# A macaron block on one core: the norms' shift moved to GpSimd, weight statistics on TensorE, and a new order of the slots

## The reference, cut to what matters

```
x: 16 x 256 x 256 f32
def layernorm(x): return (x - mean) / sqrt(var + 1e-5)              # over the last 256
def ternary(w):   scale = mean(|w|) + 1e-8; return clip(round(w/scale), -1, 1) * scale
def ffn(x):       return (silu(x @ ternary(W_up).T) * (x @ ternary(W_gate).T)) @ ternary(W_down).T   # 256 -> 1024 -> 256
def attn(x):      # 16 heads of 16, rope on q and k, causal mask, softmax
    return softmax(rope(x@wq) . rope(x@wk) / 4 + mask) @ (x@wv) @ wo
x = x + 0.5 * ffn(layernorm(x))
x = x + attn(layernorm(x))
x = x + 0.5 * ffn(layernorm(x))
```

## Time and profile before

| | |
|---|---|
| median of 3 runs | 773.08 us (772.38 to 777.07) |
| the profiled execution | 772.13 us |
| its span, first to last instruction | 770.0 us |
| busy share of the span | PE 81%, DVE 79%, ACT 78%, POOL 66% |
| mean granted TensorE clock | 0.952 |

### The profile page before, as it was taken

One profiled execution on the slowest core, in us unless ns is written; L12 is line 12 of the kernel. 1 busy time (PEld: TensorE's weight loads), 2 busy tenths in 40 slices (PEclk: granted clock), 3 DMA queues, 4 the chain that ended last, 5 costly groups with the idle time before them and its releaser, 6 DMA issues. The chain is left out here.

```text
span 770.0 us, 16604 instructions
## 1 busy us (share of the span) xinstructions
PE 622.2 (81%) x5952; PEld 471.1 (61%) x5952; DVE 611.8 (79%) x1542; ACT 598.4 (78%) x1175; POOL 504.8 (66%) x440
## 2 busy tenths in 40 slices
PE   0548888768989898989898998989899696868756
PEld 0336666546767676767676776767676364646444
DVE  1857777878889998889898988888889686867643
ACT  4124578878988989888989888889899787879732
POOL 1112758766868787877868786868687767676522
PEclk9979999989999999999999999999999898989798
DMA  8500317674766666574839393947667777776520
GB/s 337 163 1 1 71 34 123 129 160 84 138 117 125 124 125 137 111 138 88 167 69 183 72 179 66 167 93 143 115 123 135 144 125 133 129 139 132 107 56 14
DMA packets 310994, 90.42 MB, mean 117 GB/s; under 512 B 301696, under 2 KB 310144, under 8 KB 310400
## 3 DMA queue, kind: packets, MB, share of 16 engines
q1 hardware_dynamic: 310336, 87.06, 58.4%
q10 hardware_dynamic: 576, 2.29, 0.8%
HBM read 9.63 MB, written 4.19 MB: 18 GB/s over the span
## 5 line engine op out<-in xcount | busy, mean ns | idle before, releaser
L1008 POOL TENSOR_TENSOR hid_l<-hid,hid_h 128x512 f16<-128x512 f32 x128 | 148.8, 1163 | 138.3 <-ACT hid_h L635 131.5
L615 ACT ACTIVATE prob<-score_ps,exp_bias,exp_scale 128x256 f32<-128x256 f32 (+1 forms) x512 | 223.9, 511 | 8.5 <-DVE exp_bias L868 8.3
L1003 POOL TENSOR_TENSOR prob_hl<-prob,prob_hl 128x768 f16<-128x768 f32 x128 | 210.7, 1646 | 26.5 <-ACT prob_hl L626 26.5
L386 PE MATMUL down_ps<-tern_down,hid_h 128*128 128x256 f16 x512 | 120.5, 275 | 22.9 <-POOL hid_l L1008 18.8
L386 PE MATMUL up_ps<-xt_hi,tern_up 128*128 128x256 f16 x512 | 128.2, 287 | 7.8 <-DVE tern_up L716 5.7
L386 PE MATMUL up_ps<-xt_lo,tern_up 128*128 128x256 f16 x512 | 127.6, 286 | 0.0
L386 PE MATMUL gate_ps<-xt_hi,tern_gate 128*128 128x256 f16 x512 | 122.7, 279 | 2.2 <-DVE tern_gate L716 1.8
L386 PE MATMUL gate_ps<-xt_lo,tern_gate 128*128 128x256 f16 x512 | 122.2, 278 | 0.0
L386 PE MATMUL down_ps<-tern_down,hid_l 128*128 128x256 f16 x512 | 120.2, 275 | 0.0
L630 ACT ACTIVATE tanh_b<-up_ps,tanh_scale 128x512 f32<-128x512 f32 x128 | 87.2, 681 | 39.7 <-PE up_ps L386 37.8
L895 DVE SCALAR_TENSOR_TENSOR silu_b<-tanh_b,up_ps 128x512 f32<-128x512 f32 x128 | 87.4, 683 | 34.4 <-ACT tanh_b L630 34.3
(11 more groups left out here) (95 smaller groups left out, 1335.9 us busy)
## 6 DMA issues: line engine op xcount, KB each, us to landing
xs<-x SPq DMA_DIRECT2D x16, 256.0 KB, 2.9
out<-xs SPq DMA_DIRECT2D x16, 256.0 KB, 3.0
raw_w<-prob_hl SPq DMA_TRANSPOSE x128, 3.8
raw_gate<-w_gate_t ACTq DMA_DIRECT2D x1, 1024.0 KB, 7.9
raw_up<-w_up_t SPq DMA_DIRECT2D x1, 1024.0 KB, 8.0
...
```

The source lines that it names most:

```text
L386: mm = pe.matmul(dst, lhs, rhs, start=flags and n == 0, stop=n == len(pairs) - 1, skip_group_check=True)
L615: e = act.activation(prob[:, n % 2, at + j * width:at + (j + 1) * width], score_ps[:, 1 - tile, j * width:(j + 1) * width], ACT.Exp, bias= ...
L1003: pool.tensor_tensor(prob_hl[:, n % 2, 1, :], prob[:, n % 2, :], prob_hl[:, n % 2, 0, :], ALU.subtract).then_inc(prob_l_done, 1)
L1008: pool.tensor_tensor(hid_l[:, n % 2, :, :].rearrange("p m n -> p (m n)"), hid[:, n % 2, :], hid_h[:, n % 2, :, :].rearrange("p m n -> p (m ...
```

## The change

Four things are changed together.

1. The shift moves from DVE to POOL, as two instructions of 128x1, behind the norm's power and ahead of `hidden_lo`.
2. The sums over the partitions are products with a matrix of ones on PE; the maxima are turned by a PE transpose, reduced on DVE, put on a diagonal and spread by another product. POOL has no PARTITION_ALL_REDUCE any more. `split_weights_hi` moves from DVE to ACT.
3. The weights are loaded in halves, one half on SP's queue and one on ACT's, in the order up, gate, down, attention weights. Before, up and down were on SP's queue and gate and the attention weights on ACT's.
4. Tables and written orders: the ramp starts a slot earlier with one more round (`FIRST_FFN` -16, `AHEAD` 7), qk0 moves from slot 1 (b) to slot 0 (b), v from slot 3 (b) to slot 4 (b), the norms' steps are redistributed, `exp_biases` stands ahead of `pv_add` and `row_max` ahead of `pv_scale` on DVE, `tanh` ahead of `norm_apply` on ACT, `turn_probs` ahead of `store` on SP, and the g < 0 orders of all engines are new.

```diff
-FIRST_FFN = -15
-AHEAD = 6
+FIRST_FFN = -16
+AHEAD = 7
...
-OF_BATCH = [("norm2", -8, "a"), ("qk0", -7, "b"), ("qk1", -6, "a"), ("v", -5, "b"),
+OF_BATCH = [("norm2", -8, "a"), ("qk0", -8, "b"), ("qk1", -6, "a"), ("v", -4, "b"),
...
-    1: {"stats": 4, "mean": 4, "var": 2, "power": 2, "shift": 1, "apply": 1},
-    2: {"stats": 2, "mean": 2, "var": 2, "power": 2, "shift": 1, "apply": 1},
-    3: {"stats": 2, "mean": 2, "var": 2, "power": 1, "shift": 0, "apply": 0},
+    1: {"stats": 4, "mean": 3, "var": 3, "power": 3, "shift": 2, "apply": 1},
+    2: {"stats": 3, "mean": 3, "var": 2, "power": 2, "shift": 2, "apply": 1},
+    3: {"stats": 2, "mean": 1, "var": 1, "power": 1, "shift": 1, "apply": 0},
...
-            sp.dma_start(raw_up[:, :], w_up_t).then_inc(up_loaded, 16)
-            sp.dma_start(raw_down[:, :], w_down_t).then_inc(down_loaded, 16)
+            sp.dma_start(raw_up[:, 0:HID], w_up_t[:, 0:HID]).then_inc(up_loaded, 16)
+            sp.dma_start(raw_gate[:, 0:HID], w_gate_t[:, 0:HID]).then_inc(gate_loaded, 16)
             sp.dma_start(rows(1), x_dram[1]).then_inc(x_loaded[1], 16)
+            sp.dma_start(raw_down[:, 0:HID], w_down_t[:, 0:HID]).then_inc(down_loaded, 16)
...
+            def sum_weight(n):
+                pe.wait_ge(abs_done, n + 1)
+                pe.matmul(weight_sums[n], ones, abs_sum[:, n:n + 1], start=True, stop=True).then_inc(sums_done, 1)
...
+            def turn_maxima():
+                pe.wait_ge(wmax_done, 1)
+                pe.transpose(w_max_row, w_max[:, :], ident_f[:, :]).then_inc(wmax_turned, 1)
+            def spread_maxima():
+                pe.wait_ge(wdiag_done, 2)
+                pe.matmul(w_max_all, ones[0:4, :], w_diag[:, :], start=True, stop=True).then_inc(wmax_all, 1)
...
-            def norm_shift(k, b):
-                dve.wait_ge(rstd_done[k], b + 1)
-                dve.scalar_tensor_tensor(out=shift[k][:, :, None], in0=mv[k][:, :, 0:1], scalar=-1.0,
-                                         in1=rstd[k][:, :, None], op0=ALU.mult, op1=ALU.mult).then_inc(shift_done[k], 1)
...
+            def norm_shift(k, b):
+                pool.wait_ge(rstd_done[k], b + 1)
+                for tile in range(NT):
+                    s = pool.tensor_scalar(shift[k][:, tile:tile + 1], mv[k][:, tile, 0:1], rstd[k][:, tile:tile + 1], -1.0,
+                                           ALU.mult, ALU.mult)
+                s.then_inc(shift_done[k], 1)
...
-            def sum_all():
-                pool.wait_ge(abs_done, 2)
-                pool.partition_all_reduce(abs_sum_all[:, 0:2], abs_sum[:, 0:2], P, RADD).then_inc(abs_all, 1)
...
-            def max_all():
-                pool.wait_ge(wmax_done, 1)
-                pool.partition_all_reduce(w_max_all[:, :], w_max[:, :], P, RMAX).then_inc(wmax_all, 1)
```

More of the change, by code:

```diff
@@ L158, in uses_of, with run_slots @@
     return MISC_AT.get((slot, place), [])
-def run_slots(engine_slot, before={}):
+def run_slots(engine_slot, before=()):
     for g in range(FIRST_SLOT, LAST_SLOT + 1):
-        if g in before:
-            before[g]()
+        for at, part in before:
+            if at == g:
+                part()
         engine_slot(g)
@@ L520, in slot @@
                         up(*r)
-                    for n in pair_of(g, 0):
-                        scores(n)
                     for name, b in uses_of(g, "a"):
@@ L526, in slot @@
                         product_v(n)
+                    for n in pair_of(g, 0):
+                        scores(n)
+                    for r in round_of(g, 0):
+                        gate(*r)
                     for name, b in uses_of(g, "b"):
                         misc(name, b)
-                    for r in round_of(g, 0):
-                        gate(*r)
                     for r in round_of(g, 1):
@@ L955, in slot @@
                         norm_stats(k, b)
+                    for n in pair_of(g, 3):
+                        pv_add(n)
                     for n in round_numbers(g, 0):
```

248 lines of the change are left out of this document (143 added, 105 removed).

## The result

The changed kernel takes 730.51 us (median of 4 runs, 726.7 to 730.72) against 774.48 for the kernel before on the same chip; the ratio is 0.9419, 95% interval 0.9374 to 0.9465. The forecast was 723.5, in a range of 706 to 744. The profiled execution took 730.72, with a span of 728.9 for 770.0 and a granted clock of 0.956 for 0.952.

The account below looks back on a forecast made before the run. No engine alone bounds the kernel; how evenly slots are filled counts. Slot 0 at 85 + 68 to slot 14 + 520.6 to slot 126 + 46.8 tail = 720.4 span; 722.5 profiled, 723.5 median forecast, range 706 to 744.

Parts of the forecast that it names:

- rival 1: Slots 0 and 4: new waits mean spreading the projections gives nothing; 14 us more, 737; chance 0.2.
- signs of being wrong: Full batch: PE waiting for hid_l in slot 7 or ACT for v in slot 4 over 0.3, or slot 0 over 5.6.
- About 0.9 and some of slot 0's 0.35: Slots 7 and 0: the part of the 2.15 us saved per full batch put down to the shift's place.
- I cost it at nothing: Slots 6 and 7: hid_l some 1.1 us later behind POOL's shift, covered by PE's spare 1 us; uncovered, 1.1 per batch.
- Rival 2: POOL's small instructions are dear, 1.4 for two, uncovered in two slots a batch: 33 us more, 756; chance 0.08.
- Rival 3: POOL becomes the pace, each of 128 slots late by 0.5 us: 64 us more, 787; chance 0.03.
- Tanh and PE's load end as late in most: Slots' loop: reason for counting no gain from exp_bias ahead of pv_add, which is 0.2 us in bare slots.
- rival 4: Better than counted: exp_bias's 0.2 in every slot (128 x 0.1 to 0.2) and the ramp at 82: 705; chance 0.12.
- The maxima's term: Ramp: PE's 10.06 us wait around POOL's reduction goes, the chain in its place costs 1: -9.
- -6.5: Ramp, first product: -3 from the earlier load, -3.8 from no longer waiting for other sums, PE's sums +0.3.
- rival 5: Ramp: loading by halves does nothing, as both queues feed the same engines; 3 us, 726; chance counted within the forecast's 0.57.
- 1.8 less per batch: Light stage: saving from the new places of v and qk0, a little under the full stage's; light batches at 36.0.

Follow-up runs that it names:

- e4: Changed kernel with qk0 and v back at their old places (slots 1 and 3): 746.82 us, ratio 0.9648.
- e12: Kernel before with qk0 and v at their new places and norm1's var and power a slot earlier, nothing else: 767.68 us, ratio 0.9913.
- e11: Changed kernel with POOL's shift instructions issued twice, the second pair into tensors nobody reads: 734.72 us, ratio 0.9481.
- e1: Kernel before with only the shift moved to POOL, right behind the norm's power: 765.76 us, ratio 0.9876.
- e5: Kernel before with only norm1's var and power a slot earlier, the shift staying on DVE: 757.51 us, ratio 0.9783.
- e3: Changed kernel with the shift back on DVE, at its old place and old leads: 727.83 us, ratio 0.9396.
- e10: The early up weights of e9 put on the kernel of e3, with the shift on DVE: 724.65 us, ratio 0.9357.
- e9: Changed kernel with up's sum and ternary weights a slot earlier and batch 1's rows loaded ahead of the gate's half: 726.08 us, ratio 0.9367.
- e6: Changed kernel with pv_add ahead of exp_biases again in the slots from 0 on: 737.61 us, ratio 0.9539.
- e2: Kernel before with only the sums and maxima over the partitions moved to PE: 766.39 us, ratio 0.9891.
- e8: Changed kernel with the weights loaded whole again instead of in halves: 730.70 us, ratio 0.9436.
- e7: Changed kernel with AHEAD at 6 again, the ramp still starting at slot -16: 735.16 us, ratio 0.9501.

## Why the prediction was right, and where it was off

**The full stage: right.** From slot 14 to 86 the forecast was 345.6, measured 345.5. Every slot is within 0.11 of its forecast, so the 0.3 a batch added for waits lies mostly in the first two of the nine batches (39.8 from slot 14, 38.7 from 22, then 38.1 to 38.4). The spreading of the two projections gives what was worked out (e4: 16 us, by rival 1's count 14), and rival 1's new wait in slot 0 didn't come. It seems to hang on ACT's written order, in which the norm went behind the copy. I had priced this only for remainder 5. With the old order, in e12, slot 0 takes 6.32 ("or if slot 0 of a batch is longer than 5.6"), while slot 4 keeps its 4.91: half of rival 1. The link to ACT's order is read from rows, as said at e12.

**Two of my signs of being wrong came all the same.** PE waits 0.90 for `hid_l` in slot 7 and ACT 0.60 for v in slot 4, both "by more than 0.3". Neither made its slot longer than forecast (4.66 for 4.65, 4.91 for 4.85): the first had "1 us to spare", and the second was in the 4.85 as "ACT's second exponentials wait for v's copy". The signs contradicted the sum; the length of a slot would have been the right one. That the first wait had almost no room left is shown by e11.

**The shift: the loss was right, the remedy was not.** "About 0.9 and some of slot 0's 0.35 come from the shift's place" put down to the engine what the leads do. The wait and the collision are real and go with the shift's move (e1). But they go with norm1's leads as well (e5, more than in e1), and with the new leads the engine is worth nothing (e3 against the changed kernel, e10 against e9: both 1 to 3 us to DVE's side, within the intervals). The forecast was not harmed, since the change has both: the number is right here by luck, as the reason given for it is not the one that the runs show.

**POOL's small instructions: a size off.** I took 0.3 for the pair, measured 0.50 (265 ns each in the median, 1.58 for a pair beside DVE's w_lo in e1), inside the bounds of 0.2 to 1.4 in the median; the longest pair of the changed kernel, in the ramp beside DVE's `tern_down` of 128x2048, takes 2.53 (28.25 to 30.78). "I cost it at nothing" held, but only just: by e11 the next 0.5 us costs 0.47 in each batch. Rival 2's price would have applied in one slot of a batch, not in two. Rival 3's does not: twice the shifts cost 4 us in all.

**exp_bias: the nothing held, not its reason.** "Tanh and PE's load end as late in most" is true of six slots of a full batch and of half the slots of a light one; elsewhere e6 shows the bias to be in the loop, and its place is worth 7 us. Remainder 6 came out at the 3.66 of before for another reason: `exp_biases` ahead of `pv_add` takes one instruction out from between the maxima and the bias, and `row_max` ahead of `pv_scale`, a part of the same change, puts one in (the rows at e6). The two were not priced together. So rival 4, 0.1 to 0.2 in every slot, didn't come.

**The ramp: 2.6 too early** (87.60 for 85). The maxima's term held: -9 forecast, and e2, with the sums, gave -8.1. The first product came at 18.92 where -6.5 from 23.01 is 16.5, 2.4 late. Of the parts of the -6.5, the earlier load came to 2.25 us for 3 (first sum at 7.04), and from first sum to first product it took 11.9 for 13.7, 1.8 less where I had 3.5 ("the first product no longer waits" for the other sums, 3.8, less 0.3). What stood there instead is DVE, which makes `tern_up` behind the statistics of batch 1 and waits 8.22 for their rows; the gate's sum, ahead of the product in PE's order, is over by 14.42 and holds nothing up. e9 takes the rows' wait away; only then the gate's sum is what the product waits for, and slot 0 follows by 2.75. The two last terms, +3.7 for one slot more and -3 for the split on ACT and the shifts, have no run of their own: the -8.1 of e2 and the 4.1 at the first product leave about -0.2 of the 12.3 for both together, where I had +0.7. Loading by halves gives the 1.5 us of e8 at that product and nothing that the time shows, which is rival 5.

**AHEAD: not priced apart.** Costed as a shift of rounds at 0.7 each, slots 0 to 14 were 68.5 for 68. e7 shows that it gives about 5 us, part of it with PE's clock in slots 8 to 14, which a price by the round doesn't have.

**The last stage: 4.1 too short**, the largest error (179.1 for 175.0, by a trace that can be 3 off, as e8 shows). The term that was too large is the "1.8 less per batch": from slot 94 on three batches take 0.85 less each than before, and e4 puts the whole stage's gain from the places at 2.0. A light batch takes 35.2 to 37.7 and not 36.0, 145.8 for the four, since qk0 makes slot 0 dearer there (5.26 for 4.10) and remainders 4 and 5 take 4.1 to 4.2 and 4.8 to 5.0 for 3.6 and 4.5 before. The last one takes 33.2 for 31. There DMA comes in: PE and SP in slots 116 and 117 of the changed kernel,

```profile
639.08 3.37 SPq L370 DMA_TRANSPOSE k_pad<-k_row  x1
...
646.29 0.53 PE L451 MATMUL pv_ps<-v_row,raw_w 128*128 128x33 f16 x12 [2.06 <-DMA raw_w<-prob_hl]
```

The transpose of `k_pad` takes 3.37 us here and 1.72 a few slots on; the probabilities' transposes queue behind it, PE waits 2.06, and the slot takes 6.20, where others of remainder 5 take 4.8 to 5.0. In slot 120 PE waits 1.58 for the same transposes. PE's clock isn't it: the granted clock of slot 117 is 0.52, and in the kernel before it is 0.50 and the slot takes 4.47. The traces show that the long slot 117 goes with the places of qk0 and v: the five kernels with the old places have 4.5 to 4.9 there (e4 4.47), the nine with the new ones 4.7 to 6.5. Nor is a slow transpose of `k_pad` special to this stage: in the kernel before, 8 of the 32 take 2.2 to 3.5 us for a median of 1.7. Why single ones are slow is open; no run was about it.

**The tail** took 48.2 for 46.8, with no reason that I have shown. The granted clock is 0.82 there for 0.87, but e11 has 48.6 at 0.89, so the clock alone doesn't explain it. The four errors, 2.6, 0.5, 4.1 and 1.4 (and -0.1 in the full stage), make up the 8.5 by which the span was off 720.4. The profiled run stands 1.8 above its span, for 2.13, and 0.2 above the median, where 0.95 below it was assumed.
